# Attention scores of a two-layer graph kernel: plain float32, two heads in the two row halves of the array

## The reference, cut to what matters

```
h = relu(layernorm(x));  x = x + relu(self(h) + sum over edges of rel(h)[type, src])
h = relu(layernorm(x));  Q, K, V = split(h @ W_qkv.T + b_qkv)        # 8 heads of 64
score(e, head) = Q[dst(e), head] . K[src(e), head] / sqrt(64)
att = softmax of score over the edges that end in one node
x = x + (sum over edges of att * V[src]) @ W_ff.T + b_ff
```

## Time and profile before

| | |
|---|---|
| median of 3 runs | 365.79 us (365.73 to 365.95) |
| profiled execution, span from first to last instruction | 364.6 us |
| TensorE busy | 310.8 us, 85% |
| VectorE busy | 222.5 us, 61% |
| ScalarE busy | 143.3 us, 39% |
| GpSimd busy | 71.8 us, 20% |
| mean granted clock of TensorE | 0.976 |

### The profile page before, as it was taken

One profiled execution on the slowest core, in us unless ns is written; L12 is line 12 of the kernel. 1 busy time (PEld: TensorE's weight loads), 2 busy tenths in 40 slices (PEclk: granted clock), 3 DMA queues, 4 the chain that ended last, 5 costly groups with the idle time before them and its releaser, 6 DMA issues.

```text
span 364.6 us, 7072 instructions
## 1 busy us (share of the span) xinstructions
PE 310.8 (85%) x2604; PEld 262.3 (72%) x2604; DVE 222.5 (61%) x493; ACT 143.3 (39%) x276; POOL 71.8 (20%) x90
## 2 busy tenths in 40 slices
PE   1006999996998799999999999999799999999940
PEld 1006888884787677876878788999688888888830
DVE  3068999999869333353345783585867575656310
ACT  1025243223015134225333451667877474747300
POOL 5032051528005000337000340130001010101010
PEclk9999999999699899999999999999999999999995
DMA  6703003030300300000260000000000000000000
GB/s 191 237 18 118 3 3 119 3 120 0 118 4 4 118 2 2 2 1 11 108 230 2 1 0 2 0 2 1 0 4 0 31 2 29 3 31 0 31 5 22
DMA packets 7303, 14.35 MB, mean 39 GB/s; under 512 B 598, under 2 KB 614, under 8 KB 7258
## 3 DMA queue, kind: packets, MB, share of 16 engines
q1 hardware_dynamic: 6900, 13.17, 11.0%
q10 hardware_dynamic: 358, 0.57, 0.5%
HBM read 12.46 MB, written 1.28 MB: 38 GB/s over the span
## 4 chain that ended last, share of the span: by engine, by line
PE 76%; DVE 6%; DMA 6%; issue 4%; ACT 3%; PEldq 1%; POOL 1%; DVEq 0%; SPq 0%; POOLq 0%; ACTq 0%
PE banks L1095 24%; PE banks L1081 8%; PE banks L1041 7%; PE banks L959 7%; PE banks L1172 7%; PE banks L1158 6%; PE banks L1147 6%; DMA xs<-in_x_dram 5%; PE banks L1192 4%; DVE src_hot L714 2%; PE banks L998 1%; DMA raw<-in_L_gnn_W_qkv_dram 1%; PE banks L1182 1%; PE banks L1071 1%; PE banks L1027 1%
## 5 line engine op out<-in xcount | busy, mean ns | idle before, releaser
L714 DVE TENSOR_SCALAR src_hot<-iota,edge_keys 128x640 f16<-128x640 f16 x120 | 58.0, 536 | 0.0
L959 PE MATMUL banks<-dst_hot,src_hot 128*128 128x96 f16 x600 | 32.0, 216 | 30.1 <-DVE src_hot L714 22.9
L959 PEld LDWEIGHTS banks<-dst_hot,src_hot 128*128 128x128 f16 x600 | 29.3, 103 | 34.7 <-issue 34.4
L1095 PE MATMUL banks<-w_hl,hT 128*128 128x512 f32 x180 | 46.7, 409 | 0.0
L372 POOL TENSOR_TENSOR w_hl<-raw,w_hl 128x512 fp32r<-128x512 f32 x24 | 32.0, 1357 | 72.9 <-ACT w_hl L441 72.9
L877 DVE CUSTOM_DVE_ANT_0 s_sb<-banks,mask_add 128x640 f32<-128x640 f32 x40 | 32.6, 822 | 22.2 <-PE banks L1147 22.1
L576 ACT ACTIVATE p_sb<-s_sb,neg_max 128x640 f32<-128x640 f32 x40 | 32.9, 823 | 17.3 <-DVE neg_max L877 17.3
L1095 PEld LDWEIGHTS banks<-w_hl,hT 128*128 128x128 f32 x180 | 33.8, 195 | 7.2 <-DVE hT L743 0.3
L450 ACT ACTIVATE adjT<-banks 128x480 f16<-128x480 f32 x20 | 11.4, 569 | 61.4 <-PE banks L973 61.4
L1041 PE MATMUL banks<-adjT,h 128*128 128x320 f16 x240 | 35.1, 306 | 0.4 <-DVE zT_even L767 0.4
L1041 PEld LDWEIGHTS banks<-adjT,h 128*128 128x128 f16 x240 | 23.4, 100 | 10.1 <-DVE zT_even L767 0.7
(11 more groups left out here) (143 smaller groups left out, 467.6 us busy)
## 6 DMA issues: line engine op xcount, KB each, us to landing
raw<-in_L_gnn_W_self_dram SPq DMA_DIRECT2D x3, 1024.0 KB, 15.5
raw<-in_L_gnn_W_rel_dram SPq DMA_DIRECT2D x3, 1024.0 KB, 5.4
raw<-in_L_gnn_W_qkv_dram SPq DMA_DIRECT2D x3, 1024.0 KB, 5.4
xs<-in_x_dram SPq DMA_DIRECT2D x1, 1024.0 KB
raw<-in_L_gnn_W_ff_dram SPq DMA_DIRECT2D x1, 1024.0 KB, 5.2
out_dram<-ybuf SPq DMA_DIRECT2D x4, 256.0 KB, 2.0
bv_rows<-in_L_gnn_b_qkv_dram ACTq DMA_DIRECT2D x1, 256.0 KB
bff_rows<-in_L_gnn_b_ff_dram ACTq DMA_DIRECT2D x1, 256.0 KB
```

The lines of the kernel that those rows point to most:

```text
L714: nc.vector.tensor_scalar(src_hot[:, par, k, :], iota[:, 0, :], edge_keys[:, 0, bass.ds(c + k, 1)], None, ALU.is_equal).then_inc(s_src[par ...
L959: ins = mm(banks[:, w % 2, jt * R * WIN:(jt + 1) * R * WIN], src_hot[:, par, k, jt * P:(jt + 1) * P], dst_hot[:, par, k, :], start=(first ...
L1095: ins = mm(to, lhs[:, pl, kt, it * P:(it + 1) * P], weights[:, pw, kt, c0:c0 + cn], start=(start and n == 0), stop=(n == 3 * KD - 1), skip ...
```

## The change

The 128 rows of the array are used as two halves of 64. Head 2a of a pair takes rows 0 to 63 and head 2a + 1 rows 64 to 127, which is how `k` and `q` units lie in partitions already. ScalarE writes queries and keys as plain float32 (`q_f`, `k_f`), and all splits and copies go. A score step is a pair of heads: 4 matmuls of 64 rows, in plain float32, with 320 columns each, half outside and head inside. The four banks now hold one pair, so pair m waits for both reductions of pair m - 1, and one semaphore increment at the end of a pair releases both its reductions. In the order, pair m stands at 2m; nothing else moves.

```diff
-        q_st = place("q_st", o_z0, [P, H, NP], F32R)
-        k_hi = place("k_hi", o_z0 + 20480, [P, H, NP], F32R)
-        k_lo = place("k_lo", o_z0 + 40960, [P, H, NP], F32R)
+        q_f = place("q_f", o_z0, [P, KD, NP], F32)
+        k_f = place("k_f", o_z0 + 10240, [P, KD, NP], F32)
-        qk_f = place("qk_f", o_ss, [P, 2, NP], F32)
...
         for n in range(NT * H):
-            placed += [(n, "score", n), (n + 0.1, "smax", n), (n + 0.7, "exp", n)]
+            placed += [(n + 0.1, "smax", n), (n + 0.7, "exp", n)]
+        placed += [(2 * m, "score", m) for m in range(NT * KD)]
...
-                    ins = nc.scalar.activation(qk_f[:, n % 2, half * HALF:(half + 1) * HALF], bank(u)[:, 0:HALF],
-                                               ACT.Identity, bias=bqk[:, n:n + 1],
+                    ins = nc.scalar.activation((q_f if kind == "q" else k_f)[:, a, half * HALF:(half + 1) * HALF],
+                                               bank(u)[:, 0:HALF], ACT.Identity, bias=bqk[:, n:n + 1],
...
-                    dve.wait_ge(s_sc, n + 1)
+                    dve.wait_ge(s_sc, n // 2 + 1)
...
-                    if n == 1:
-                        split_q(KD - 1)
...
                 if kind == "score":
-                    it, h = divmod(n, H)
...
-                    if n >= 2:
-                        pe.wait_ge(s_smax, n - 1)
+                    it, a = divmod(n, KD)
+                    if n < KD:
+                        pe.wait_ge(s_uhi, act_done[("q", a, 1)])
+                    if n >= 1:
+                        pe.wait_ge(s_smax, 2 * n)
                     for half in range(2):
                         cols = slice(half * HALF, (half + 1) * HALF)
-                        for p, k in enumerate((k_hi, k_lo)):
-                            ins = mm(banks[:, 2 * (n % 2) + half, 0:HALF], q_st[:, h, it * P:(it + 1) * P],
-                                     k[:, h, cols], start=(p == 0), stop=(p == 1))
+                        for hh in range(2):
+                            me = slice(64 * hh, 64 * hh + 64)
+                            ins = mm(banks[:, 2 * hh + half, 0:HALF], q_f[me, a, it * P:(it + 1) * P],
+                                     k_f[me, a, cols], start=True, stop=True)
                     ins.then_inc(s_sc, 1)
```

More of the change, by code:

```diff
@@ L197, in gnn_kernel @@
         s_mask = sem("s_mask")
[L198 to L202, removed]
         s_sc = sem("s_sc")
@@ L294, in gnn_kernel @@
         attention = [(kind, n) for _, kind, n in sorted(placed, key=lambda step: step[0])]
[L297 to L303, removed]
         WINDOW_CHUNKS, BOUNDS, EDGE_KEYS, MASKS, BIASES = 6, 9, 10, 16, 18
@@ L404, in _ @@
                 nc.gpsimd.tensor_tensor(xs[:, it, :], xs[:, it, :], bff_rows[:], ALU.add).then_inc(s_xb, 1)
[L406 to L414, removed]
             for n in range(NT * KD):
@@ L500, in unit_part @@
                     n = a if kind == "k" else KD + a
-                    if n == 0:
+                    if u == ("k", 0, 0):
                         act.wait_ge(s_keys, BIASES)
-                    if n >= 2:
-                        act.wait_ge(s_qk, split_count(n - 1))
-                    ins = nc.scalar.activation(qk_f[:, n % 2, half * HALF:(half + 1) * HALF], bank(u)[:, 0:HALF],
-                                               ACT.Identity, bias=bqk[:, n:n + 1],
+                    ins = nc.scalar.activation((q_f if kind == "q" else k_f)[:, a, half * HALF:(half + 1) * HALF],
+                                               bank(u)[:, 0:HALF], ACT.Identity, bias=bqk[:, n:n + 1],
                                                scale=-SCALE if kind == "q" else 1.0)
@@ L552, in _ @@
                 unit_part(u)
[L553 to L567, removed]
             for step in attention:
@@ L788, in unit_part @@
                     nc.vector.tensor_tensor(v_sb[:, jt, :], b, bv_rows[:], ALU.add).then_inc(s_ufree, 1)
[L789 to L792, removed]
                 else:
                     nc.vector.engine_nop().then_inc(s_ufree, 1)
[L795 to L822, removed]
             dve.wait_ge(s_keys, EDGE_KEYS)
```

## The result

The changed kernel takes 371.03 us (median, 370.45 to 371.46) against 365.87 us for the kernel before beside it: 1.0135 times, 95% interval 1.0113 to 1.0157. It is 5.2 us slower; forecast were 7.7 us and 373.5 us. The profiled span went from 364.6 to 368.9 us.

The account below looks back on a forecast made before the run. TensorE's own time was taken to bound the steady attention. Terms of -1.6, +6.6, +1.0 and +1.7 us gave +7.7 us on a 364.6 us span, 372.3 us, plus 1.2 us for the median: 373.5 us, range 367.5 to 381 us.

Parts of the forecast that it names:

- Nothing is gained beside TensorE: Splits, copies and semaphores on other engines: dropping them saves nothing at the end, except one stall at the attention's start.
- the `split_q` stall: Start of the attention: the last query split holds VectorE for 1.67 us ahead of smax 2, and so score 4.
- Streams, -1.6 us: Score matmuls on TensorE: a pair takes 1.09 us for 1.17, saving 0.08 us for each of 20 pairs.
- two readings: Plain float32 records in `pv`: either 0.109 us each with array halves side by side, or 0.054 us with no overlap.
- reading one: Records of `pv`: each takes 0.109 us, 0.85 ns a column, and the array's left and right halves run side by side.
- Changes of division, +6.6 us: TensorE's order in the attention: 79 changes of the array's division against 46, 33 more at 0.2 us each.
- Steady waits, +1.0 us: Steady attention: waits for the previous pair's reductions show behind pairs 8, 12 and 16, 0.3 us each, and a little elsewhere.
- The start, +1.7 us: First pairs of the attention: uncovered waits for reductions cost 1.7 us more than before, net of the `split_q` stall.
- the clock rival: Start of the attention: holes behind pairs 0 and 1 lower TensorE's clock, about 5 us, 378.5 us; chance 7%.
- The not-slower rival: The 33 changes: entering and leaving row halves costs nothing, 366.9 us, or 365.0 with loads running ahead; chance 9%.
- the overlap rivals: Pairs in row halves: halves overlap badly, 378.9 us, chance 18%; or not at all, 395 us, chance 14%.
- the signs named at the end: Changed profile: eight paired records, 0.27 us apart; 20.1 us rounds; waits behind every fourth pair; start holes of 2.1 and 1.4 us.

Follow-up runs that it names:

- experiment 3: The changed kernel with all 128 rows in each score matmul, so no row halves (does not compute the reference): 387.23 us, 1.0584 times the kernel before.
- experiment 2: The kernel before with its pv steps in twos and rb directly ahead of them, 20 changes of division for 46: 361.76 us, 0.9901.
- experiment 7: The changed kernel with pair 1 in banks 4 to 7, and pv and rb directly ahead of a pair where no three turns result: 366.03 us, 1.001.
- Experiment 9: The changed kernel with pair 1 in banks 4 to 7, pv in twos and rb directly ahead of them, 56 changes of division: 371.37 us, 1.0145.
- experiment 5: The changed kernel with each pv and rb directly ahead of a score pair, 60 changes of division for 79: 370.76 us, 1.0148.

## Why the prediction was right

**Nothing is gained beside TensorE.** Right. VectorE, ScalarE and GpSimd are 20, 11.5 and 5 us lighter and the `k` and `q` block stands at 28.16 for 28.17 us. The one credit, the `split_q` stall, is inside the start term.

**Streams, -1.6 us.** Right in mechanism and size. A pair takes 1.08 us for 1.09 forecast; two scores before take 8 x 0.147 = 1.17; saved about 0.10 x 20 = 1.9 us. Without overlap the pair would be the 2.15 us of experiment 3. The prediction said that the trace of before left two readings. It did not: in narrow windows the records of a `pv` start two by two, the first two at 277.02, the next at 277.18 and then every 0.11 us, which is reading one, the halves side by side.

```profile
277.02 0.33 PE L1172 MATMUL banks<-pT,v_sb 128*64 128x128 f32 x2
277.18 0.39 PE L1172 MATMUL banks<-pT,v_sb 128*64 128x128 f32 x4
277.29 0.39 PE L1172 MATMUL banks<-pT,v_sb 128*64 128x128 f32 x4
```

**Changes of division, +6.6 us.** Right mechanism, price somewhat too high: 33 changes cost about 5.5 us, 0.17 each, for 0.2. Single records of both traces from 271 us on, read in narrow windows as above, give the price by what comes behind the change:

| change | us |
|---|---|
| into column halves (`pv`, `rb`) | 0.14 |
| into row halves (a pair) | 0.20 |
| out of either to a turn | 0.15 to 0.16 |
| out to a score or to `ff` | 0.20 |

Draining is 0.09 to 0.10 us in all of them. What differs is how much longer the first distance behind it is, which I take for the exposed part of the load: 0.05 to 0.06 us ahead of column halves and of a turn, 0.10 us ahead of the others. So the forecast's 0.19 us for entering row halves was right. Wrong was to put 0.2 on every change: it had itself halved the exposed load of 64 columns, and it took a full 0.11 us for the load of a turn, where half of that is exposed. The row for it stood in the earlier trace rows: four turn loads take 0.42 us behind a `pv`. A single one is 0.14 us long and two usual distances are 0.22, so the second is only 0.06 us behind the first. The prices add up in a round: ten changes before make 1.65 us, 17 after make 2.80, four pairs save 0.39, and 2.80 - 1.65 - 0.39 = 0.76 us, as measured. The averages of experiments 2 and 7, 0.143 to 0.147 us, are net of the short waits named there.

**Steady waits, +1.0 us.** Wrong in size: zero. A round of 19.50 us has no idle time. My account gave 4.7 us of VectorE against 4.4 of TensorE behind pair 8. VectorE's timeline there:

```profile
287.08 0.82 DVE L804 CUSTOM_DVE_ANT_0 s_sb<-banks,mask_add 128x640 f32<-128x640 f32 x1 [1.90 <-PE banks L1068]
289.05 0.69 DVE L838 TENSOR_TENSOR ybuf<-banks,xs 128x512 f32<-128x512 f32 x1 [1.14 <-PE banks L1113]
289.65 0.68 DVE L812 COPY pT<-banks 128x512 f32<-128x512 f32 x1
290.25 0.81 DVE L804 CUSTOM_DVE_ANT_0 s_sb<-banks,mask_add 128x640 f32<-128x640 f32 x1
```

The steps start 0.60 us apart, not 0.69, as each begins before the one ahead is through. The last reduction ends at 291.06, and pair 9's first load comes at 291.20, 0.31 us behind the turn ahead of it, as at any change. It is just in time, by less than can be read. Experiment 9 shows that the mechanism exists: with two turns alone between two pairs it costs 1.25 us at once.

**The start, +1.7 us.** Right in mechanism, and near in size. 2.83 us are lost up to `rb` 0. Nine more changes there make 1.5 us, the streams nothing (six pairs for eleven heads), which leaves 1.3 us for the waits. The two holes behind pairs 0 and 1 and the wait ahead of turn 3 all came where they were written out.

**Sum.** -1.9 + 5.5 + 0 + 1.3 = 4.9 us against 4.8 in the traces. Of the 7.7 us forecast, 1.1 too many are in the changes and 1.0 in the steady waits, 0.4 in the start and 0.3 in the streams; all four errors point the same way, so the total is not right by luck of opposite errors. The timed runs have 5.2 and 5.7 us; what goes beyond the traces is not resolved run by run, but a fall of the clock at the start, seen in one of two profiles, adds 1.0 us to executions in which it happens. So the clock rival, held apart in the forecast, adds to the likeliest case. The not-slower rival is refuted by experiment 7, the overlap rivals by experiment 3. Of the signs named at the end these held: a round between 18.8 and 23 us, eight records for a pair, two by two and 0.27 us apart, and the two holes at the start. A wait behind every fourth pair did not come; so, and by the lower price of the changes, the round is 19.50 us for 20.1.

## What to carry to other kernels

Count the changes of the array's division in TensorE's order before counting columns: where TensorE has no idle time, each cost 0.14 to 0.20 us here, by what is loaded behind it, and steps of one division put side by side saved that without touching a matmul (experiment 2). Look then for the short waits that the new order makes; they took back part of the gain in experiments 2, 5, 7 and 9. A form that takes load from VectorE, ScalarE and GpSimd gained nothing here under a full TensorE. Where steps are made coarser (pairs for heads), ask how many buffers are left: four banks with one pair in them turned a wait of two heads' distance into one that opens holes wherever the order has under about two us of other work between pairs (in experiment 9, 0.9 us of turns and 1.25 us of waiting). And read single records in narrow windows before leaving two readings open.

## What the runs showed of the hardware that was not expected

Plain float32 with 64 rows overlaps between row halves without measurable loss: 1.08 us for eight records, against 2.15 us on all rows. The Trainium skill's "TensorE: Matmul & The Clock Gate", Measured speedup vs the span model, gives 3.07 times for four row tiles; here two halves gave 2.15 / 1.08 = 2.0 times, and the loss that I had derived from it did not come.

A change of the array's division costs 0.14 to 0.20 us: 0.09 to 0.10 us of draining in every case, and a longer first distance, by 0.05 to 0.06 us ahead of column halves and of plain float32 transposes, by 0.10 us ahead of row halves, float32r scores and `ff`.

Behind a hole of 1.77 us in TensorE's work the granted clock stood at the lower level for 3.4 us, from 257.6 us on, in one execution, and not in another of the same kernel with the same hole.
